# Expert selector, query and key weights loaded and split inside cross attention

## The reference, cut to what matters

```
x = x + tanh(g_xattn[0]) * xattn(layernorm(x), ctx, ctx, mask)        # 16 heads of 16, 361 context rows
x = x + tanh(g_ffn[0])  * ffn(layernorm(x))

ffn(x):                                   # x [32, 100, 256]
  gate_v = top2 gate of sigmoid(x @ sel_v_w.T)       # 64 logits: 8 heads x 8 experts
  gate_o = top2 gate of sigmoid(x @ sel_o_w.T)       # 64 more
  q = x @ q_w.T ; k = x @ k_w.T                      # [256 -> 1024] each, 8 heads of 128
  v = sum over experts of gate_v * (x @ v_w[h, e])
  att = softmax(q k^T / sqrt(128)) ; ctx = att v
  out = sum over experts of gate_o * ctx @ o_w[h, e]
```

## Time and profile before

| | before |
|---|---|
| time, median of 3 runs | 1933.88 us (1932.85 to 1934.6) |
| the profiled execution: span from first to last instruction | 1928.9 us |
| PE busy | 1873.3 us, 97% |
| DVE busy | 1496.2 us, 78% |
| ACT busy | 1135.1 us, 59% |
| POOL busy | 935.0 us, 48% |
| DMA, mean over the span | 90 GB/s |

### The profile page before, as it was taken

One profiled execution on the slowest core, in us unless ns is written; L12 is line 12 of the kernel. 1 busy time (PEld: TensorE's weight loads), 2 busy tenths in 40 slices (PEclk: granted clock), 3 DMA queues, 4 the chain that ended last, 5 costly groups with the idle time before them and its releaser, 6 DMA issues. The chain is left out here.

```text
span 1928.9 us, 57544 instructions
## 1 busy us (share of the span) xinstructions
PE 1873.3 (97%) x13454; PEld 1146.6 (59%) x13454; DVE 1496.2 (78%) x4309; ACT 1135.1 (59%) x3591; POOL 935.0 (48%) x1368
## 2 busy tenths in 40 slices
PE   6899999999997999999999999999999999999998
PEld 3688888888875555444444445545555555555543
DVE  6788888888887962555555556658999999999989
ACT  3688888888885444444444445445555555555543
POOL 4022222222212012666666666666677676776767
PEclk9999999999998999999999999999999999999999
DMA  6678887888752484000000022122222222222201
GB/s 156 127 116 119 118 120 118 120 120 118 119 87 93 205 330 181 27 27 27 14 27 27 27 85 94 52 64 71 71 80 67 79 75 71 79 69 77 75 13 66
DMA packets 192148, 174.22 MB, mean 90 GB/s; under 512 B 51921, under 2 KB 183378, under 8 KB 190034
## 3 DMA queue, kind: packets, MB, share of 16 engines
q1 hardware_dynamic: 189906, 165.06, 37.9%
q0 software_dynamic: 2176, 8.39, 1.3%
HBM read 112.41 MB, written 60.98 MB: 90 GB/s over the span
## 5 line engine op out<-in xcount | busy, mean ns | idle before, releaser
L1489 POOL TENSOR_TENSOR o_side<-o_side,o_tmp 128x256 f32 (+1 forms) x528 | 396.2, 750 | 196.6 <-POOL o_side L1489 70.5
L1258 PE MATMUL e_pv<-e_vw,e_xhi 128*128 (+1 forms) x1600 | 475.9, 379 | 1.2 <-ACT e_out L1181 1.2
L1191 ACT ACTIVATE big<-e_pv,gates 128x128 f32<-128x128 f32 x800 | 228.6, 369 | 280.1 <-PE e_pv L1258 278.5
L654 ACT ACTIVATE c_ex<-c_sm,c_nmax 100x361 f32<-100x361 f32 x512 | 302.7, 593 | 58.0 <-DVE c_nmax L537 49.5
L1617 ACT ACTIVATE o_tmp<-o_py,gates 128x256 f32<-128x256 f32 x528 | 222.3, 475 | 194.1 <-PE o_py L1689 123.3
L1689 PE MATMUL o_py<-o_whi,a_chi 128*128 128x512 f16 x800 | 304.9, 381 | 0.1
L1689 PE MATMUL o_py<-o_wlo,a_chi 128*128 128x512 f16 x800 | 304.5, 381 | 0.0
L1689 PE MATMUL o_py<-o_whi,a_clo 128*128 128x512 f16 x800 | 304.3, 380 | 0.0
L1258 PE MATMUL e_pv<-e_vw,e_xlo 128*128 (+1 forms) x800 | 303.2, 379 | 0.0
L537 DVE CUSTOM_DVE_ANT_0 c_sm<-c_ps,c_mbias 100x361 f32<-100x361 f32 x512 | 269.0, 527 | 38.4 <-PE c_ps L739 32.6
L1124 DVE TENSOR_SCALAR e_acc<-e_pv,gates 128x128 f32<-128x128 f32 x400 | 121.8, 346 | 225.9 <-PE e_pv L1258 225.8
(11 more groups left out here) (164 smaller groups left out, 3213.4 us busy)
## 6 DMA issues: line engine op xcount, KB each, us to landing
qk<-e_out SPq DMA_DIRECT2D x16, 1600.0 KB, 5.2
c_kst<-k_parts SPq DMA_DIRECT2D x256, 90.2 KB, 4.9
a_q<-qk SPq DMA_DIRECT2D x64, 200.0 KB, 2.4
a_k<-qk SPq DMA_DIRECT2D x64, 200.0 KB, 2.4
v<-e_out SPq DMA_DIRECT2D x20, 640.0 KB, 3.3
a_v<-v SPq DMA_DIRECT2D x64, 200.0 KB
c_ctx<-in_ctx_t SPq DMA_DIRECT2D x32, 361.0 KB, 3.5
e_wst<-in_v_w POOLq DMA_DIRECT2D x8, 1024.0 KB, 7.6
```

The lines of the kernel that those rows point to most:

```text
L654: act.activation(ex[:, h % 4, 0:SK], sm[:, h % 4, :], ACT.Exp, scale=-1.0, bias=nmax[:, h % 4:h % 4 + 1], accum_out=den[:, b.par, HEAD[h]: ...
L1191: act.activation(tmp[:, hh, e, :], p_v[:, hh, 1, e * PD:(e + 1) * PD], ACT.Copy, scale=gate).then_inc(s_av, 1)
L1258: last = pe.matmul(p_v[:, hh, half, :], a[:, c, bass.ds(t * P, P)], vw[:, bass.ds(col + (w * DC + c) * VW, 512)], start=j == 0, stop=j == ...
L1489: pool.tensor_tensor(side[:, x.t, :], side[:, x.t, :], tmp[:, slot(x, r), j, :], ALU.add).then_inc(s_pool, 1)
```

## The change

The buffers and semaphores of the selector and the two weights are made before cross attention (`router_weights`), so that they live through both stages. SP loads all three in cross attention, behind its body of batch 1. GpSimd splits them in the bodies of the last four batches: the selector in batch 28, and two of eight parts in each batch, with three instructions a part (high half, scale in place, subtract). The splits on ACT and DVE in the experts stage are gone; PE waits on GpSimd's counter, and the two loops of projections become one. ACT evaluates one square root at the end of cross attention and one sigmoid behind the experts stage's square root, both into values that nobody reads.

```
 def stage_cross(...):
+            def load_router():
+                sp.dma_start(f.sst[:, :, :], sel_t.rearrange("(c p) e -> p c e", p=P)).then_inc(f.s_loaded, 16)
+                for w, src in enumerate((q_t, k_t)):
+                    sp.dma_start(f.wst[:, w, :, :], src.rearrange("(c p) n -> p c n", p=P)
+                                 ).then_inc(f.s_loaded, 16)
+
+            def body_and_router(b):
+                body(b)
+                if isinstance(b.n, int) and b.n == 1:
+                    load_router()
...
-                batches(sp, body)
+                batches(sp, body_and_router)
...
+            def split_router(n):
+                w, part = divmod(n, PARTS)
+                src = f.wst[:, w, :, part * PART:(part + 1) * PART]
+                cut = slice(w * H * PD + part * PART, w * H * PD + (part + 1) * PART)
+                pool.wait_ge(f.s_loaded, 48)
+                pool.tensor_scalar(f.qkhi[:, :, cut], src, WS, None, ALU.mult).then_inc(f.s_high, 1)
+                pool.wait_ge(f.s_high, n + 2)
+                pool.tensor_scalar(src, src, WS, None, ALU.mult).then_inc(f.s_scaled, 1)
+                pool.wait_ge(f.s_scaled, n + 2)
+                pool.tensor_tensor(f.qklo[:, :, cut], src, f.qkhi[:, :, cut],
+                                   ALU.subtract).then_inc(f.s_low, 1)
+
             def body(b):
                 bias_x(b)
                 if later(b, 1):
                     widen_mask(later(b, 1))
                 if later(b, 3):
                     split(later(b, 3))
+                if isinstance(b.n, int) and b.n >= NB - 4:
+                    if isinstance(b.n, int) and b.n == NB - 4:
+                        split_selector()
+                    for n in range(2):
+                        split_router(2 * (b.n - NB + 4) + n)
...
                 copy_rt(last)
+                act.wait_ge(s_rt, NB)
+                act.activation(warm[:, :], rt[:, 0:1], ACT.Sqrt)

 def stage_experts_in(...):
-            sp.dma_start(sst[:, :, :], sel_t.rearrange("(c p) e -> p c e", p=P)).then_inc(s_sel, 16)
             sp.dma_start(rsb[:, :], rs.partition_broadcast(P)).then_inc(s_rs, 16)
-            sp.dma_start(wst[:, 0, :, :], q_t.rearrange("(c p) n -> p c n", p=P)).then_inc(s_wq, 16)
-            sp.dma_start(wst[:, 1, :, :], k_t.rearrange("(c p) n -> p c n", p=P)).then_inc(s_wk, 16)
...
             act.activation(std[:, :], mv[0:SQ, :, 1], ACT.Sqrt).then_inc(s_std, 1)
-            act.wait_ge(s_sel, 16)
-            act.activation(shi[:, :, :], sst[:, :, :], ACT.Copy, scale=WS).then_inc(s_whi, 1)
+            act.wait_ge(s_std, 1)
+            act.activation(f.sst[0:SQ, 0, 0:1], std[:, 0:1], ACT.Sigmoid)
...
-            for part in range(2):
-                pe.wait_ge(s_wlo, 2 + part)
-                with pe.Fori(part * H, (part + 1) * H) as u:
+            pe.wait_ge(f.s_low, SPLIT)
+            with pe.Fori(0, 2 * H) as u:
```

More of the change, by code:

```diff
@@ L323, in stage_queries, with stage_cross @@
         return programs
-def stage_cross(nc, k, sems, queries, cross, x, ctx_t, mask, q_parts, k_parts, big, mv, x1):
+def stage_cross(nc, k, sems, queries, cross, f, x, ctx_t, mask, q_parts, k_parts, big, mv, x1, sel_t, q_t, k_t):
     LAG_T, LAG_C, LAG_E, LAG_A = 3, 4, 3, 5
@@ L896, in stage_experts_in @@
         pick1 = k.gates[:, :].rearrange("p (g e) -> p g e", e=E)
[L897 to L900, removed]
+        wst, qkhi, qklo, shi, slo = f.wst, f.qkhi, f.qklo, f.shi, f.slo
         std, rstd, half = (m.sbuf(n, [SQ, NB]) for n in ("e_std", "e_rstd", "e_half"))
@@ L948, in stage_experts_in @@
         QF = 4
-        PARTS = NB // 8
+        SPLIT = 9
         def sync(sp):
@@ L1048, in vector @@
                     x_lo(t - 2)
[L1049 to L1053, removed]
             x_lo(NB - 2)
             x_lo(NB - 1)
[L1056 to L1061, removed]
             def spread(v):
@@ L1164, in scalar @@
                     probabilities(n)
[L1165 to L1172, removed]
             for n in (*logit_tiles(NB - 1), *logit_tiles(NB)):
@@ L1233, in tensor @@
             pe.wait_ge(s_p, NT)
-            for part in range(2):
-                pe.wait_ge(s_wlo, 2 + part)
-                with pe.Fori(part * H, (part + 1) * H) as u:
[L1237 to L1244, removed]
+            pe.wait_ge(f.s_low, SPLIT)
+            with pe.Fori(0, 2 * H) as u:
+                for w in range(NC):
+                    pe.wait_ge(s_qe, NC * u + w + 1)
+                    tok = slice(w * NW, (w + 1) * NW)
+                    for n, (c, a, b) in enumerate((c, a, b) for c in range(DC)
+                                                  for a, b in ((qkhi, xhi), (qkhi, xlo), (qklo, xhi))):
+                        last = pe.matmul(p_q[:, w % QF, 0:NW], a[:, c, bass.ds(u * PD, PD)],
+                                         b[:, c, tok], start=n == 0, stop=n == 3 * DC - 1)
+                    last.then_inc(s_qk, 1)
             pe.wait_ge(s_qe, QF + 2 * H * NC)
@@ L1758, in constants, with router_weights @@
     return k
+def router_weights(nc, ctx, sems):
+    f = Constants()
+    m, held = Store(nc, ctx), Store(nc, sems)
+    f.wst = m.sbuf("e_wst", [P, 2, DC, H * PD])
+    f.qkhi, f.qklo = (m.sbuf(f"e_qk{n}", [P, DC, 2 * H * PD], F16) for n in ("hi", "lo"))
+    f.sst = m.sbuf("e_sst", [P, DC, P])
+    f.shi, f.slo = (m.sbuf(f"e_s{n}", [P, DC, P], F16) for n in ("hi", "lo"))
+    f.s_loaded, f.s_high, f.s_scaled, f.s_low = (held.sem(f"e_s_w{n}") for n in ("load", "high", "scale", "low"))
+    return f
 def cross_inputs(nc, ctx):
@@ L1796, in flamingo @@
             mv = m.sbuf("x1_mv", [P, NB, 2])
-            with ExitStack() as innermost, ExitStack() as sems:
+            f = router_weights(nc, inner, sems)
+            with ExitStack() as innermost, ExitStack() as own:
                 c = cross_inputs(nc, innermost)
-                queries = stage_queries(nc, k, sems, c, big, x, g_xattn, g_ffn, wq, bq, ctx_t, (wk, wv, wo), (bk, bv, bo), q_parts)
-                cross = stage_cross(nc, k, sems, queries, c, x, ctx_t, mask, q_parts, k_parts, big, mv, x1)
+                queries = stage_queries(nc, k, own, c, big, x, g_xattn, g_ffn, wq, bq, ctx_t, (wk, wv, wo), (bk, bv, bo), q_parts)
+                cross = stage_cross(nc, k, own, queries, c, f, x, ctx_t, mask, q_parts, k_parts, big, mv, x1, sel, qw, kw)
                 stage_attention_in(nc, queries, cross)
-            e = stage_experts_in(nc, k, sems, big, mv, sel, qw, kw, vw, rs, qk, v)
+            e = stage_experts_in(nc, k, sems, f, big, mv, vw, rs, qk, v)
         o = stage_attention_out(nc, k, sems, e, x1, qk, v, ow, y)
```

23 lines of the change are left out of this document (17 added, 6 removed).

## The result

The changed kernel takes 1946.22 us (median of 5, 1944.44 to 1947.5), the kernel before in the same session 1933.88 (5 runs, 1930.22 to 1935.65): ratio 1.0067, 95% interval 1.0055 to 1.008, slower by 12.3 us. The forecast was 1936.0 with a range up to 1941.5: wrong. The profiled execution spans 1944.4 us, 15.5 more than that of before, which was a quick one of its kind.

The account below looks back on a forecast made before the run. PE, busy for 97% of the span, was taken as the bound. The seam's -5.55, the load's +3.8 and +1.9 and the splits' +2.0 summed to +2.15 us on 1933.88: 1936.0, range 1929.5 to 1941.5.

Parts of the forecast that it names:

- The seam: Where cross attention ends and the experts stage begins: five terms that together give back 5.55 us.
- terms 1 to 4: At the seam: square root table -0.9, sigmoid table -0.55, ACT's e_qkhi pieces -1.4, DVE's two e_qklo -1.3 us.
- term 5: Ahead of the projections: with most of PE's pause gone, the clock no longer falls to half, -1.4 us.
- The tables: At the seam: square root and sigmoid tables loaded earlier on ACT, -0.9 and -0.55 us.
- the pause: PE's 2.08 us idle before the projections: without DVE's two e_qklo PE starts earlier, -1.3 us.
- Rival C: Seam: GpSimd's normalisation sets the tiles' pace and the clock still falls; seam gives 2.75, time 1938.8 us; chance 0.1.
- The load: Batch 2 of cross attention: moved loads delay batch 3's mask, PE stalls +3.8 us, then half clock costs +1.9.
- the 1.9 us of gaps: DMA engines taken as 0.42 full for 3 us after 111, leaving 1.9 us free for the moved loads.
- The port: Last batches of cross attention: DVE's copies, such as c_rdx, wait when they meet GpSimd's splits, +2.0 us.
- Rival B: Queue in batch 2 decides: stall 6.9, clock 2.5, splits 3.0, seam gives 5; time 1941.3 us; chance 0.17.

Follow-up runs that it names:

- e2: The changed kernel without GpSimd's splits and without the early tables, its three loads still in batch 2: 1941.27 us, ratio 1.0044 to the kernel before.
- e15: The kernel before with one one-column memset added on DVE ahead of the last stage: 1932.58 us, ratio 0.9999.
- e1: The kernel before with only the two early table loads (square root and sigmoid) added: 1932.02 us, ratio 0.9994.
- e13: The kernel before with its three loads at the kernel's start and the two early tables, no GpSimd split, two projection loops: 1933.26 us, ratio 1.0002.
- e14: The kernel before with 13 one-column memsets on DVE behind the two e_qklo, nothing else: 1938.76 us, ratio 1.0029.
- e11: The changed kernel with three one-column memsets added on DVE behind the last e_xlo: 1938.68 us, ratio 1.0032 to the kernel before.
- e8: e3 with GpSimd's splits at the kernel's start too and none in the last four batches: 1943.8 us, ratio 1.0048 to the kernel before.
- e9: e3 with three one-column memsets added on DVE behind the last e_xlo: 1933.18 us, ratio 1.0003 to the kernel before.
- e3: The changed kernel with its three loads issued at the kernel's start, splits and tables as in the change: 1938.8 us, ratio 1.0027 to the kernel before.

## Why the prediction was wrong

1. *The seam* (-5.55): about right in size, in part by luck. The stretch holds terms 1 to 4, -4.15, and shrank by 3.8 us; that it should shrink by 5.5 was a slip, as term 5 falls behind the first projection. The clock gave 1.4 there (the first 300 matmuls take 50.9 us and not 52.3), of which the changed kernel kept 0.6: 4.4 in its trace, 5.2 without the wait for `e_out`. The tables gave 0.8 and 1.7 in two kernels where 1.45 was forecast; the pause went from 2.08 to 0.66 us (-1.3 forecast). But the pause doesn't settle the clock, as term 5 has it: it is 2.08 us in e2 and e15 too, and the clock stays at 1.00; in before, e1, e13 and e14 it falls. None of the nine kernels with 0.66 us falls. Rival C is out. PE's first projection and the window behind it in e15:

```profile
620.04 0.34 PE L1245 MATMUL e_pv<-e_xhi,e_qkhi 128*128 128x400 f16 x1 [2.08 <-DVE e_qklo L1059]
```

```profile
620.00:625.00 5.00, 4.96 (x30) 2.90 (x31) 5.00 (x3) 2.01 (x4) 1.60 (x2) 1.00 0.66 227
```

2. *The load* (+3.8 and +1.9): the mechanism was right, the sizes too small. The stall is 4.79 us and not 3.8, and 6.25 in e11, where the clock didn't fall in batch 2; the clock costs 3.0 us (5.96 of work at 0.50) and not 1.9. That is over the bound of 2.5, for which the earlier trace rows ends too soon: the clock was low for 6.9 us there as here, but PE worked in only 5.2 of them. e2 prices both with all that hangs on them at 8.5 us by its ratio, 6.2 to 10.8 by the interval, against my 5.7. The step that failed is the 1.9 us of gaps in the queue from 111 to 114, which I took off: the engines were at 1.06 until 116. From the issue of batch 0's store to the landing of the last of batch 3's queries it is 6.4 us before (107.03 to 113.45) and 12.6 after (108.78 to 121.41), 6.2 more, and 6.7 in e11: nearly all of the 6.5 us of full engines, with no gap. And I had timed the mask, with 0.76 us of slack; the queries gate PE, and have 0.3 (landed at 113.45, first score of batch 3 at 113.76).

```profile
113.76 0.32 PE L739 MATMUL c_ps<-c_kst,c_qst 128*100 128x361 f16 x1
```

```profile
120.36 0.53 PE L783 MATMUL c_ps<-c_kst,c_qst 128*100 128x361 f16 x1 [6.25 <-DMA c_qst<-q_parts]
```

3. *The port* (+2.0 in the last batches): not resolved. The last four periods of cross attention are 62.5 to 63.5 us in seven kernels without a split there and 62.5 to 65.6 (mean 64.2) in nine with them, but e8, which has none there, shows 64.3. `c_rdx` itself, which I had named as the victim, took 0.29 to 0.53 us in the last four batches of the changed kernel. The split's operations took what the earlier trace rows has (1.49, 1.50 and 1.16 us a part), 32 us in all and not 37.
4. *The last stage* (nothing forecast): +9.1 us, the largest miss, and the second step that failed: the sum held only what the diff names and put the rest at nothing without a reason. 6.0 us are DVE's code, three instructions shorter; e9 and e11 give them back. The rest is in the first two periods (24.7 to 25.4 us in before, e1, e2, e13 and e14, and 25.9 to 28.4 in the others but e15): there the clock did not fall at the stage's start, PE came sooner to the point where it waits for the next head's weights, and waited longer for a transfer that doesn't depend on it. Before, then after (ACT, PE):

```profile
1301.09 0.63 ACT L1633 ACTIVATE o_whi<-o_wst  x1 [2.07 <-DMA o_wst<-in_o_w]
...
1304.28 1.11 PE L1669 MATMUL a_pc<-a_ext,a_v 100*128 100x100 f32 x8 [2.13 <-issue]
```

```profile
1309.09 0.63 ACT L1651 ACTIVATE o_whi<-o_wst  x1 [5.32 <-DMA o_wst<-in_o_w]
...
1312.31 2.00 PE L1687 MATMUL a_pc<-a_ext,a_v 100*128 100x100 f32 x8 [5.41 <-issue]
```

   The longer wait alone costs nothing. What costs is that the weights come later (`o_whi` starts 15.8 us behind the first `a_ps` and not 14.2) and that behind the wait the clock is at 0.50 for some 6.9 us and not 3.5:

```profile
1305.30:1308.80 3.50, 3.50 (x10) 1.25 (x10) 2.36 (x7) 1.81 (x5) 1.33 (x2) 0.51 0.19 59
```

```profile
1312.20:1319.00 6.80, 6.69 (x20) 3.62 (x21) 4.69 (x13) 3.04 (x11) 2.25 (x3) 0.50 0.11 31
```

   What keeps the clock up at the stage's start in these kernels is open; e15, one memset from before, is among them. Its clock falls at neither place, and its two periods take 23.0 us, the least of all.

In sum: loads 8.5, seam -4.4 to -5.2, DVE's code 6.0, first periods 1 to 3, splits 0 to 2, against 12.3 measured. Rival B (slower, through the queue) had the direction; it ended at 1941.3, which is the time of e2 and not of the change.

## What to carry to other kernels

Price a load that is moved by the transfer that stands behind it in the same queue, and by who waits for that first; in the idle time at the kernel's start these loads cost some 1.5 us by the ratios (e13 over e1, within the noise) and not e2's 8.5. Where these two instructions of DVE and GpSimd meet, who starts first keeps its time and the other pays 0.5 us, so 0.1 us of phase was worth 6 us over a loop: look at such pairs in all loops behind the edit, not only at the edited ones. And before an edit is judged, run it once with the number of instructions on each busy engine restored: three dummy instructions were half of this verdict.

## What was not expected of the hardware

- Three one-column memsets on DVE ahead of a stage change its length by 6.0 us (535.98 to 529.91, e3 and e9; 535.91 to 529.91, after and e11). The stretch repeats to 0.1 us among kernels of one sort.
- The time from the end of `o_whi` on ScalarE to the start of `o_wlo` on DVE is 0.27 or 0.38 us for the same instructions, by kernel, and 0.20 in another copy of the same loop body.
- After a pause of 2.1 us at the start of the last stage the clock falls to 0.50 in five kernels (before, e1, e2, e13, e14) and stays at 1.00 in the other twelve, with the same values stage ahead of it. Ahead of the projections a pause of 2.08 us is followed by 0.50 in four kernels and by 1.00 in two (e2, e15).
